# A slot of two heads: attention scores in three passes over halves of the array's rows, queries of both heads in two buffers

## The chip, the cores and the metric

The kernel runs on one core of a Trainium2 chip. The metric is the device time of one execution in microseconds (us), lower is better. All work of the core is done by five engines with queues of their own: TensorE (PE; its weight loads are listed as PEld), VectorE (DVE), ScalarE (ACT), GpSimd (POOL) and SyncE (SP), which here starts most of the DMAs. They wait for each other with semaphores.

## What is computed

One layer of a language-model tower on 8 rows of 512 token numbers. A token's vector comes from a codebook of 2048 rows through a two-layer network (256 to 1024 to 256), so the kernel builds a table of all 2048 rows once. Then for each of the 8 batch rows (cut from the reference; layer norms run over 256 channels, the first 128 are `tok`, the others `pos`):

```python
q, k, v = x_pos @ Wq, x_pos @ Wk, x_tok @ Wv          # 16 heads of 64, 4 heads of keys and values
q = rotate(q, q_phase_angle)                           # a fixed angle for each head
att = q @ k.T / 8 + exp(alibi_log_slopes) * (i - j)    # causal: i >= j
e = exp(att - max(att))
out = (e / (1 + sum(e))) @ v
h = h + out @ Wo
y = layernorm(h)
h = h + gelu((y @ U1) @ V1 + b1) @ U2 @ V2 + b2        # ranks 64, inner width 1024
```

Everything is float32. To keep that precision with the faster `float32r` type, most products split an operand into a high part (rounded to float32r by a copy on ACT) and a low part (the rest, by a subtraction on DVE), called `_hi` and `_lo` here.

## The kernel before

`token_table` builds the table (the first 134 us of the profiled execution). `layer` does the rest: 8 batch rows times 16 heads make 128 head slots, and `SLOTS` adds a few for what lags behind. The order of the work is written out by hand: each engine's program is a loop over slots that calls the same helpers, and lists (`first`, `second`) say which products besides attention fall into which slot: `q` (queries of a pair of heads), `k` (keys for four heads), `x` (turning the positions of the next batch row), and of the batch row before `w` (output product, four tiles of tokens), `y` (turning the normed rows), `u`, `f`, `g`, `d` (the four products of the feed-forward).

A head's scores form a lower triangle of 512 x 512: four tiles of 128 queries against 128, 256, 384 or 512 keys, named by `q` = 0 to 3, in the units `UNITS = ((3,), (2, 0), (1,))`. The steps for a head:

1. `scores` on TensorE, two passes for each tile over all 128 rows. The rows of `q_both` hold the high part of the head's queries in one half and the low part in the other; `k_hi` and `k_lo` hold the keys twice. Units take turns in banks 0 and 1 of PSUM (`RING`, `ring_opened`).
2. `least_of` on DVE (L994) adds mask and position term, writes the result to `probs` and keeps each row's least. `probs` is a ring of three heads.
3. `exps` on ACT (L822), with the sums; `invert` on DVE (L1001); `normalize` on POOL (L783) multiplies all four tiles by the reciprocal.
4. `turn` on TensorE (L1372), ten transposes into banks 2 to 4 (`turn_ps`, one buffer), two slots behind the scores (`LAG`); `move` on ACT (L829) copies them to `turned_sb`.
5. `values` on TensorE (L1388), for two heads at once, in column halves of the array (`tile_position=(0, e * D)`), float32, into bank 5; `o_part` on ACT (L871) and `o_rest` on DVE (L1040) split the result.

Banks 6 (`a_bank`) and 7 (`c_bank`) serve all other products; `before` and `emptied` make each use wait until the one before it has been read. ACT must load another table when it goes from exponentials to gelus and back, which is once a batch row each way. In the text, switching the division of the array means going between products over the whole array, products in column halves and products in row halves. The line numbers in the profile are those of this listing.

## Time and profile before

| | us |
|---|---|
| median of 3 runs | 945.58 |
| lowest, highest | 944.63, 945.79 |
| the profiled execution | 943.51 |
| its span, first to last instruction | 941.7 |
| of it before the first scores | 134 |

The mean granted clock of TensorE was 0.996 of 2.4 GHz. A timeline row gives start, duration, engine, source line, operation and output<-inputs; the shape stands at its end. Recorded durations of TensorE overlap each other, so its pace is read from the distances between starts. A bracket gives the engine's idle time before the row and what ended it.

### The profile page before, as it was taken

How to read it: one execution, taken by the hardware profiler on the slowest of the kernel's cores; microseconds unless marked ns; L12 is line 12 of the kernel's file. 1: busy time of each engine (PE TensorE's matmuls, PEld its weight loads, DVE VectorE, ACT ScalarE, POOL GpSimd, SP SyncE). 2: the span in 40 equal slices, each digit the busy share in tenths (PEclk: the TensorE clock that was granted, in tenths of full speed). 3: DMA queues.
4: the chain of work that ended last, by engine and by line, in shares of the span. 5: the costliest groups of instructions: out<-in, count | busy, mean ns of one | idle time of the engine just before them, and what ended most of it. 6: DMA issues, size and time to landing. Idle time of an engine off the chain costs nothing.

```text
span 941.7 us, 16997 instructions
## 1 busy us (share of the span) xinstructions
PE 872.0 (93%) x5660; PEld 680.4 (72%) x5660; DVE 581.7 (62%) x1779; ACT 728.0 (77%) x1622; POOL 627.7 (67%) x599
## 2 busy tenths in 40 slices
PE   7999978999999998999999999999899999999997
PEld 6888856777866786577766876777667866787585
DVE  5565636776684658475847575756756684658434
ACT  6855348998689869996889688877888689869843
POOL 6000069899686878688767878596868686868630
PEclk9999999999999999999999999999999999999999
DMA  9333360001000200020000100010001000000000
GB/s 262 73 112 112 125 190 1 1 1 56 2 1 1 79 1 2 1 73 7 2 1 24 56 1 1 23 58 1 1 23 57 1 1 1 23 2 1 1 23 23
DMA packets 23605, 33.56 MB, mean 36 GB/s; under 512 B 2608, under 2 KB 20176, under 8 KB 23520
## 3 DMA queue, kind: packets, MB, share of 16 engines
q1 hardware_dynamic: 19760, 19.01, 6.3%
q0 software_dynamic: 3760, 13.48, 5.0%
q8 instruction: 46, 0.75, 0.3%
q14 instruction: 39, 0.32, 0.1%
HBM read 17.80 MB, written 14.68 MB: 34 GB/s over the span
## 4 chain that ended last, share of the span: by engine, by line
PE 49%; ACT 13%; POOL 11%; issue 8%; DVE 6%; DMA 0%; POOLq 0%; DVEq 0%; ACTq 0%
PE ps L1388 12%; PE ps L1192 12%; POOL probs L783 9%; PE ps L1372 8%; PE ps L1360 5%; ACT probs L822 5%; PE ps L1361 4%; ACT turned_sb L829 4%; PE ps L1340 3%; DVE probs L994 2%; POOL token_rows L771 2%; PE ps L1200 1%; ACT k_hi L844 1%; ACT q_both L839 1%; PE ps L1334 1%
## 5 line engine op out<-in xcount | busy, mean ns | idle before, releaser
L783 POOL TENSOR_SCALAR probs<-probs,sums 128x512 f32<-128x512 f32 (+3 forms) x512 | 545.2, 1083 | 155.0 <-DVE sums L1001 154.6
L994 DVE CUSTOM_DVE_ANT_0 probs<-ps,causal,slope 128x512 f32<-128x512 f32 (+3 forms) x512 | 260.0, 547 | 162.0 <-PE ps L1361 161.5
L822 ACT ACTIVATE probs<-probs 128x513 f32<-128x513 f32 (+3 forms) x512 | 283.8, 556 | 34.9 <-DVE probs L994 27.4
L829 ACT ACTIVATE turned_sb<-ps 128x1280 f32<-128x1280 f32 x128 | 157.1, 1228 | 59.3 <-PE ps L1372 59.2
L1360 PE MATMUL ps<-k_hi,q_both 128*128 128x512 f32 (+3 forms) x512 | 181.0, 354 | 19.2 <-DVE probs L994 18.3
L1372 PE MATMUL ps<-ident,probs 128*128 128x128 f32 x1280 | 162.1, 274 | 5.3 <-POOL probs L783 5.3
L1388 PE MATMUL ps<-turned_sb,token_rows 128*64 128x512 f32 (+3 forms) x1024 | 152.0, 438 | 13.5 <-ACT turned_sb L829 13.5
L1361 PE MATMUL ps<-k_lo,q_both 128*128 128x512 f32 (+3 forms) x512 | 152.6, 324 | 0.0
L1372 PEld LDWEIGHTS ps<-ident,probs 128*128 128x128 f32 x1280 | 143.7, 142 | 6.8 <-POOL probs L783 6.5
L1388 PEld LDWEIGHTS ps<-turned_sb,token_rows 128*64 128x64 f32 x1024 | 75.2, 136 | 98.6 <-issue 82.6
L1360 PEld LDWEIGHTS ps<-k_hi,q_both 128*128 128x128 f32 x512 | 96.6, 189 | 61.1 <-DVE probs L994 34.9
L1361 PEld LDWEIGHTS ps<-k_lo,q_both 128*128 128x128 f32 x512 | 97.2, 190 | 4.6
L822 ACT ACTIVATION_READ_ACCUMULATOR probs<-probs 128x1 f32 x512 | 96.0, 188 | 0.0
L1009 DVE TENSOR_TENSOR q_both<-ps,q_both 64x512 fp32r<-64x512 f32 x128 | 88.1, 688 | 9.6 <-ACT q_both L839 6.2
L839 ACT ACTIVATE q_both<-ps 64x512 fp32r<-64x512 f32 x128 | 75.3, 588 | 14.5 <-PE ps L1192 12.8
L261 POOL TENSOR_TENSOR row_guess<-row_var,minus_half 128x4 f32<-128x4 f32 x4 | 4.1, 1026 | 89.8 <-DVE row_var L367 89.8
L1192 PE MATMUL ps<-wo_hi,o_hi 128*128 128x256 f32 x224 | 63.1, 282 | 0.0
L1192 PE MATMUL ps<-wo_lo,o_hi 128*128 128x256 f32 x224 | 62.7, 280 | 0.0
L1192 PE MATMUL ps<-wo_hi,o_lo 128*128 128x256 f32 x224 | 62.7, 280 | 0.0
L1040 DVE TENSOR_TENSOR o_lo<-ps,o_hi 128x512 fp32r<-128x512 f32 x64 | 44.2, 691 | 20.6 <-ACT o_hi L871 19.8
L310 ACT ACTIVATE hid<-ps,b_col 128x512 f32<-128x512 f32 x32 | 22.0, 686 | 28.9 <-PE ps L489 27.5
L415 DVE TENSOR_TENSOR hid_lo<-hid,hid_hi 128x512 fp32r<-128x512 f32 x32 | 22.1, 692 | 34.7 <-ACT hid_hi L315 23.4
(225 smaller groups left out, 1443.9 us busy)
## 6 DMA issues: line engine op xcount, KB each, us to landing
out_dram<-token_rows SPq DMA_DIRECT2D x7, 512.0 KB, 2.9
token_table<-made SPq DMA_DIRECT2D x4, 768.0 KB, 4.0
rows<-in_L_tok_codebook_dram SPq DMA_DIRECT2D x4, 512.0 KB, 9.9
w_f<-in_L_tok_W_dram SPq DMA_DIRECT2D x8, 256.0 KB, 6.1
early_rows<-made SPq DMA_DIRECT2D x4, 512.0 KB, 3.0
early_values<-xn SPq DMA_DIRECT2D x4, 512.0 KB, 3.0
token_table<-xn SPq DMA_DIRECT2D x4, 512.0 KB, 4.8
wo_f<-in_L_attn_Wo_dram POOLq DMA_DIRECT2D x1, 1024.0 KB, 10.3
```

The source lines that it names most:

```text
L783: ins = pool.tensor_scalar(at, at, recip[:, s % P_RING, q:q + 1], None, ALU.mult)
L822: act.activation(at, at, ACT.Exp, bias=least, scale=-1.0, accum_out=sums[:, s % P_RING, q:q + 1]).then_inc(exped, 1)
L829: act.activation(turned_sb[:, s % 2, :], turn_ps, ACT.Copy).then_inc(moved, 1)
L839: act.activation(q_both[at, s % 4, :], a_of("q", n, 0)[at, :], ACT.Copy).then_inc(q_high, 1)
L994: dve.tensor_tensor_reduce(out=probs[:, s % P_RING, start:end], in0=bank(unit % 2)[:, UNIT_AT[q]:UNIT_AT[q] + P * (q + 1)], in1=causal[:, ...
L1009: dve.tensor_tensor(q_both[to, s % 4, :], a_of("q", n, 0)[at, :], q_both[at, s % 4, :].bitcast(F32), ALU.subtract).then_inc(q_low, 1)
L1040: dve.tensor_tensor(o_lo[:, p % O_RING, :], o_bank, o_hi[:, p % O_RING, :].bitcast(F32), ALU.subtract)\
L1192: mm = pe.matmul(dst, w, x, start=n == 0, stop=n == len(parts) - 1)
L1360: pe.matmul(dst, w, k_hi[:, slot, 0:P * (q + 1)], start=True, stop=False)
L1361: mm = pe.matmul(dst, w, k_lo[:, slot, 0:P * (q + 1)], start=False, stop=True)
L1372: mm = pe.transpose(turn_ps[:, K_AT[k] + P * (q - k):K_AT[k] + P * (q - k + 1)], probs[:, s % P_RING, P_AT[q] + P * k:P_AT[q] + P * (k + 1 ...
L1388: mm = pe.matmul(o_bank[rows, P * k:T], v_rows[:, b % 3, k, n // REP * D:(n // REP + 1) * D], turned_sb[:, (s + e) % 2, K_AT[k]:K_AT[k] + ...
```

## The change

A slot now holds a pair of heads (`t`, 64 of them and two behind, indexed j = 0 to 7 within a batch row).

- **Scores.** The two heads of a pair are computed in the two row halves of the array (`tile_position=(e * D, 0)`), 64 rows of contraction each, into bank 0 for one head and bank 1 for the other. Each tile has three passes for each head: high by high, low by high, high by low.
- **Queries.** `q_hi` and `q_lo` hold both heads at once, so a pair has one copy on ACT and one subtraction on DVE over 128 partitions (before: two of each over 64).
- **Banks.** All units write banks 0 and 1, so a unit waits for the minima of the unit before it (both heads). `q`, `x` and some others use bank 6, the rest bank 7; `k` alternates; both halves of `d` use bank 7.
- **Order.** A slot on TensorE is: scores 0, the odd head's turn of two slots ago, `early`, scores 1, the first half of `values`, the even head's turn of the last slot, `middle`, scores 2, the second half of `values`, `late`. `probs` becomes a ring of four heads.
- **Normalizing** is cut up by units, with three reciprocals a pair; the smallest tile goes from POOL to DVE (`normalize_first`). The batch statistics are taken tile by tile after each `w`.
- **Memory.** `xn` and `scratch` now lie in the buffer `ff` of the feed-forward.

The core of the diff:

```diff
-            def scores(s, j):
-                if j == 0:
-                    pe.wait_ge(q_low, s + 1)
-                    pe.wait_ge(k_low, s // REP + 1)
-                ring_opened(("s", s, j))
-                unit = RING_NO["s", s, j]
-                for q in UNITS[j]:
-                    dst = bank(unit % 2)[:, UNIT_AT[q]:UNIT_AT[q] + P * (q + 1)]
-                    w = q_both[:, s % 4, q * P:(q + 1) * P]
-                    slot = s // REP % 2
-                    pe.matmul(dst, w, k_hi[:, slot, 0:P * (q + 1)], start=True, stop=False)
-                    mm = pe.matmul(dst, w, k_lo[:, slot, 0:P * (q + 1)], start=False, stop=True)
+            def scores(t, u):
+
+                if u == 0:
+                    pe.wait_ge(q_low, t + 1)
+                    pe.wait_ge(k_low, t // 2 + 1)
+                    if t >= 1:
+                        pe.wait_ge(biased, 2 * NT * t)
+                    if t >= 1 and burst(t - 1):
+                        pe.wait_ge(ff_made, KF * (t // PAIRS - 1) + 6)
+                else:
+                    pe.wait_ge(biased, 2 * NT * t + UNIT_DONE[u - 1])
+                slot = t // 2 % 2
+                for q in UNITS[u]:
+                    for n, (w, x) in enumerate(((q_hi, k_hi), (q_lo, k_hi), (q_hi, k_lo))):
+                        for e in range(2):
+                            rows = slice(e * D, (e + 1) * D)
+                            mm = pe.matmul(bank(e)[:, UNIT_AT[q]:UNIT_AT[q] + P * (q + 1)], w[rows, t % 2, q * P:(q + 1) * P],
+                                           x[rows, slot, 0:P * (q + 1)], start=n == 0, stop=n == 2, tile_position=(e * D, 0))
                 mm.then_inc(scored, 1)
...
             def turn(s):
                 pe.wait_ge(normed, s + 1)
+                pe.wait_ge(first_normed, s // 2 + 1)
                 if s >= 1:
                     pe.wait_ge(moved, s)
...
+            def minima(t, u):
+
+                dve.wait_ge(scored, len(UNITS) * t + u + 1)
+                for q, e, of in PAIR_ORDER:
+                    if of == u:
+                        s = 2 * t + e
+                        if u == 0 and s >= P_RING:
+                            dve.wait_ge(turned, s - P_RING + 1)
...
+            def after_minima(kind, n, m):
+
+                return kind in "gyd" or kind == "k" and bank_of("k", n, m) is c_bank
...
+            def normalize_first(t):
+
+                dve.wait_ge(recip_done, len(UNITS) * t + 2)
+                for e in range(2):
+                    at = probs[:, (2 * t + e) % P_RING, P_AT[0]:P_AT[0] + P]
+                    ins = dve.tensor_scalar(at, at, recip[:, t % 2, e, SUM_AT[0]:SUM_AT[0] + 1], None, ALU.mult)
+                ins.then_inc(first_normed, 1)
...
+            for t in range(SLOTS):
+                if t < ALL_PAIRS:
+                    exps(t, 0, (0,))
+                if t >= 2:
+                    move(2 * (t - 2) + 1)
+                if t < ALL_PAIRS:
+                    exps(t, 0, (1,))
...
+                for use in early(t):
                     high(*use)
...
+                if t < ALL_PAIRS:
+                    exps(t, 1)
+                for use in middle(t):
+                    high(*use)
+                if t >= 2:
+                    o_part(t - 2)
+                if 1 <= t <= ALL_PAIRS:
+                    move(2 * (t - 1))
+                if t < ALL_PAIRS:
+                    exps(t, 2)
+                for use in late(t):
+                    high(*use)
```

and the new lists of the other products:

```python
def early(t):
    i, j = divmod(t, PAIRS)
    out = []
    if t + 1 < ALL_PAIRS:
        out.append(("q", t + 1, 0))
    if 1 <= i < B and j in (2, 3):
        out.append(("w", i - 1, 2 * (j - 2)))
    return out

def middle(t):
    i, j = divmod(t, PAIRS)
    return [({5: "y", 6: "u", 7: "d"}[j], i - 1, 0)] if 1 <= i < B and j in (5, 6, 7) else []

def late(t):
    i, j = divmod(t, PAIRS)
    out = []
    if t % 2 == 0 and t // 2 + 1 < ALL // REP:
        out.append(("k", t // 2 + 1, 0))
    if i + 1 < B and j == 3:
        out.append(("x", i + 1, 0))
...
        if j in (2, 3):
            out.append(("w", b, 2 * (j - 2) + 1))
        if j == 5:
            out.append(("y", b, 1))
        if j == 6:
...
        if j == 7:
            out.append(("d", b, 1))
    return out
```

TensorE in a plain pair, from the second pass of an even head's first tile, before:

```order
L1361 MATMUL ps<-k_lo,q_both 128x512
L1360 MATMUL ps<-k_hi,q_both 128x384 [waits biased]
L1361 MATMUL ps<-k_lo,q_both 128x384
L1360 MATMUL ps<-k_hi,q_both 128x128
L1361 MATMUL ps<-k_lo,q_both 128x128
L1192 MATMUL ps<-pos_hi,wq_hi 128x512 [waits x_high,k_low]
L1192 MATMUL ps<-pos_hi,wq_lo 128x512
L1192 MATMUL ps<-pos_lo,wq_hi 128x512 [waits x_low]
L1388 MATMUL ps<-turned_sb,token_rows 64x512 [waits moved,o_low]
L1388 MATMUL ps<-turned_sb,token_rows 64x512
L1388 MATMUL ps<-turned_sb,token_rows 64x384 x2
L1388 MATMUL ps<-turned_sb,token_rows 64x256 x2
```

and TensorE's rows after the change, from the first tile of scores 1 of such a pair:

```order
L1366 MATMUL ps<-k_hi,q_hi 128x384 [waits biased]
L1366 MATMUL ps<-k_hi,q_hi 128x384
L1366 MATMUL ps<-k_hi,q_lo 128x384 x2
L1366 MATMUL ps<-k_lo,q_hi 128x384 x2
L1366 MATMUL ps<-k_hi,q_hi 128x128 x2
L1366 MATMUL ps<-k_hi,q_lo 128x128 x2
L1366 MATMUL ps<-k_lo,q_hi 128x128 x2
L1398 MATMUL ps<-turned_sb,token_rows 64x512 [waits moved,o_low]
L1398 MATMUL ps<-turned_sb,token_rows 64x512
L1398 MATMUL ps<-turned_sb,token_rows 64x384 x2
L1379 MATMUL ps<-ident,probs 128x128 [waits moved,first_normed,normed]
L1379 MATMUL ps<-ident,probs 128x128 x9
```

A head's scores were eight passes, six of them in one piece ahead of q and the values; a pair's are now 24 instructions in three pieces, this one of twelve, and the first half of the values follows it at once, in another division of the array.

ACT around the gelus of a batch row, before (the table load and the gelus are L861, the copy of o L871, of the transposes L829):

```order
L822 ACTIVATE probs,sums<-probs 128x129 [waits biased]
L871 ACTIVATE o_hi<-ps 128x512 [waits w_full,valued]
L822 ACTIVATE probs,sums<-probs 128x257 [waits biased]
L861 ACT_TABLE_LOAD [waits ff_used]
L861 ACTIVATE ff<-ps,c_col 128x512 [waits ff_full]
L861 ACTIVATE ff<-ps,c_col 128x512 [waits ff_used,ff_full] x5
L829 ACTIVATE turned_sb<-ps 128x1280 [waits valued,turned]
L861 ACTIVATE ff<-ps,c_col 128x512 [waits ff_used,ff_full] x2
L910 ACT_TABLE_LOAD
```

and after (the copy of u's result is L852, of o L868, of the transposes L829, of k L841, the gelus L858):

```order
L852 ACTIVATE rank_both<-ps 128x512 [waits u_full]
L868 ACTIVATE o_hi<-ps 128x512 [waits w_full,valued]
L829 ACTIVATE turned_sb<-ps 128x1280 [waits valued,turned]
L822 ACTIVATE probs,sums<-probs 128x257 [waits biased] x2
L841 ACTIVATE k_hi<-ps 128x512 [waits scored,k_full]
L858 ACT_TABLE_LOAD [waits ff_used]
L858 ACTIVATE ff<-ps,c_col 128x512 [waits ff_full]
L858 ACTIVATE ff<-ps,c_col 128x512 [waits ff_used,ff_full] x7
```

The copy of the transposes stood between the gelus and stands ahead of them now, with both heads' last exponentials and the copy of k.

## Rows read from the trace of the kernel before

**Rows 1.** The page, busy time, share of the span and instructions.
```profile
PE 872.0 (93%) x5660; PEld 680.4 (72%) x5660; DVE 581.7 (62%) x1779; ACT 728.0 (77%) x1622; POOL 627.7 (67%) x599
```

**Rows 2.** The timeline, one plain pair: start, duration, engine, line, operation, idle before.
```profile
312.33 0.48 PE L1360 MATMUL ps<-k_hi,q_both 128*128 128x512 f32 x1
...
312.65 0.40 PE L1361 MATMUL ps<-k_lo,q_both 128*128 128x512 f32 x1
...
313.19 0.75 DVE L994 CUSTOM_DVE_ANT_0 probs<-ps,causal,slope 128x512 f32<-128x512 f32 x1
...
315.40 0.48 PE L1360 MATMUL ps<-k_hi,q_both 128*128 128x512 f32 x1
...
316.32 0.08 DVE L994 DVE_READ_ACCUMULATOR2_ANT probs<- 128x1 f32 x1
...
316.46 0.44 PE L1360 MATMUL ps<-k_hi,q_both 128*128 128x384 f32 x1 [0.34 <-DVE probs L994]
...
316.95 1.22 ACT L829 ACTIVATE turned_sb<-ps 128x1280 f32<-128x1280 f32 x1
...
318.31 2.38 PE L1388 MATMUL ps<-turned_sb,token_rows 128*64 128x512 f32 x16 [0.32 <-ACT turned_sb L829]
...
321.97 0.48 PE L1360 MATMUL ps<-k_hi,q_both 128*128 128x512 f32 x1
```

**Rows 3.** The timeline of TensorE alone, in the batch row after.
```profile
406.20 0.39 PE L1361 MATMUL ps<-k_lo,q_both 128*128 128x512 f32 x1
406.43 0.34 PE L1360 MATMUL ps<-k_hi,q_both 128*128 128x384 f32 x1
406.61 0.34 PE L1361 MATMUL ps<-k_lo,q_both 128*128 128x384 f32 x1
...
406.84 0.27 PE L1361 MATMUL ps<-k_lo,q_both 128*128 128x128 f32 x1
406.95 0.44 PE L1192 MATMUL ps<-pos_hi,wq_hi 128*128 128x512 f32 x1
...
407.46 0.39 PE L1192 MATMUL ps<-pos_lo,wq_hi 128*128 128x512 f32 x1
407.78 2.38 PE L1388 MATMUL ps<-turned_sb,token_rows 128*64 128x512 f32 x16
410.09 0.39 PE L1360 MATMUL ps<-k_hi,q_both 128*128 128x256 f32 x1
410.31 0.28 PE L1361 MATMUL ps<-k_lo,q_both 128*128 128x256 f32 x1
410.43 1.25 PE L1372 MATMUL ps<-ident,probs 128*128 128x128 f32 x10
411.44 0.48 PE L1360 MATMUL ps<-k_hi,q_both 128*128 128x512 f32 x1
```

**Rows 4.** The page, groups: busy, mean ns of one, then idle time before.
```profile
L783 POOL TENSOR_SCALAR probs<-probs,sums 128x512 f32<-128x512 f32 (+3 forms) x512 | 545.2, 1083 | 155.0 <-DVE sums L1001 154.6
...
L822 ACT ACTIVATE probs<-probs 128x513 f32<-128x513 f32 (+3 forms) x512 | 283.8, 556 | 34.9 <-DVE probs L994 27.4
L829 ACT ACTIVATE turned_sb<-ps 128x1280 f32<-128x1280 f32 x128 | 157.1, 1228 | 59.3 <-PE ps L1372 59.2
...
L1009 DVE TENSOR_TENSOR q_both<-ps,q_both 64x512 fp32r<-64x512 f32 x128 | 88.1, 688 | 9.6 <-ACT q_both L839 6.2
L839 ACT ACTIVATE q_both<-ps 64x512 fp32r<-64x512 f32 x128 | 75.3, 588 | 14.5 <-PE ps L1192 12.8
```

**Rows 5.** The timeline around the feed-forward's gelus, ACT and TensorE.
```profile
382.79 1.28 ACT L861 ACT_TABLE_LOAD   x1
...
384.08 2.42 ACT L861 ACTIVATE ff<-ps,c_col 128x512 f32<-128x512 f32 x4
...
384.92 1.56 PE L1340 MATMUL ps<-ff,u 128*64 128x512 f32 x4 [0.47 <-ACT ff L861]
...
391.78 0.50 PE L1360 MATMUL ps<-k_hi,q_both 128*128 128x512 f32 x1
```

More of the change, by code:

```diff
@@ L648, in layer @@
     spare = g["spare"]
[L649 removed]
+    ff = g["ff"]
     z_hi, z_lo = y_hi[:, 0, :], y_lo[:, 0, :]
@@ new lines, in _ @@
+            for t in range(SLOTS):
+                i, j = divmod(t, PAIRS)
+                if t < ALL_PAIRS:
+                    minima(t, 0)
+                if 1 <= t <= ALL_PAIRS:
+                    invert(t - 1, 2)
+                for use in late(t - 1) if t >= 1 else []:
+                    if after_minima(*use):
+                        low(*use)
+                if 1 <= i < B and j == 4:
+                    norm_front(("y", i - 1))
+                if 1 <= i < B and j == 5:
+                    norm_back(("y", i - 1))
+                for use in early(t):
+                    if use[0] == "w":
+                        low(*use)
+                if t < ALL_PAIRS:
+                    minima(t, 1)
+                    invert(t, 0)
+                for use in early(t):
+                    if use[0] != "w":
+                        low(*use)
+                if t < ALL_PAIRS:
+                    minima(t, 2)
+                    invert(t, 1)
+                    normalize_first(t)
+                for use in middle(t):
+                    low(*use)
+                if t >= 2:
+                    o_rest(t - 2)
+                for use in late(t):
+                    if not after_minima(*use):
+                        low(*use)
+                if 1 <= i < B and j == 4:
+                    norm_root(("y", i - 1))
@@ L1374, in turn, with values @@
                 mm.then_inc(turned, 1)
-            def values(s):
+            def values(s, tiles):
                 b, n = divmod(s, HEADS)
@@ L1383, in values @@
                     pe.wait_ge(o_low, s // 2)
+                if b >= 1 and n == HEADS - 6:
+                    pe.wait_ge(ff_made, KF * b)
                 pe.wait_ge(moved, s + 2)
-                for k in range(NT):
+                for k in tiles:
                     for e in range(2):
@@ L1409, in _ @@
                     filler(bank(1), 4)
-            for s in range(SLOTS):
-                if s < ALL:
-                    scores(s, 0)
-                    scores(s, 1)
-                for use in first(s):
+            for t in range(SLOTS):
+                if t < ALL_PAIRS:
+                    scores(t, 0)
+                if t >= 2:
+                    turn(2 * (t - 2) + 1)
+                for use in early(t):
                     product(*use)
-                if s == ALL:
+                if t < ALL_PAIRS:
+                    scores(t, 1)
+                if t == ALL_PAIRS:
                     last_ahead(0)
-                if 2 + LAG <= s < ALL + 1 + LAG and (s - LAG) % 2 == 0:
-                    values(s - 2 - LAG)
-                if s < ALL:
-                    scores(s, 2)
-                turn_ahead = burst(s) or ("u", s // HEADS - 1, 0) in second(s)
-                if turn_ahead and LAG <= s < ALL + LAG:
-                    turn(s - LAG)
-                for use in second(s):
-                    product(*use)
-                if not turn_ahead and LAG <= s < ALL + LAG:
-                    turn(s - LAG)
-                if s == ALL:
+                if t == ALL_PAIRS + 1:
+                    last_ahead(2, range(PAIRS // 2 - 1))
+                if t >= 2:
+                    values(2 * (t - 2), (0, 1))
+                if 1 <= t <= ALL_PAIRS:
+                    turn(2 * (t - 1))
+                for use in middle(t):
+                    product(*use)
+                if t < ALL_PAIRS:
+                    scores(t, 2)
+                if t >= 2:
+                    values(2 * (t - 2), (2, 3))
+                for use in late(t):
+                    product(*use)
+                if t == ALL_PAIRS:
                     last_ahead(1)
-                if s == ALL + 1:
-                    last_ahead(2, range(PAIRS // 2 - 1))
             last_ahead(2, range(PAIRS // 2 - 1, PAIRS - 2))
```

288 lines of the change are left out of this document (97 added, 191 removed).

## The prediction

> **What bounds the kernel now.** I read the shares first: TensorE is busy for 93% of the span, ACT 77%, DVE 62% [rows 1]. A busy share that high says only that TensorE sets the time on average, so I then read one plain pair of heads in the timeline [rows 2] and the distances between the starts of TensorE's instructions [rows 3].
>
> The distances are what counts, since recorded durations overlap. In [rows 3] a pass of 512 columns takes 0.23 us (406.20 to 406.43), one of 384 takes 0.18 (406.43 to 406.61), one of 256 takes 0.12 (410.31 to 410.43) and one of 128 takes 0.11 (406.84 to 406.95): the small ones go at the pace of their weight load, and I count both at 0.11. The ten transposes take 1.01 (410.43 to 411.44). The 16 products of `values` take 2.31 with the gap behind them (407.78 to 410.09): the two column halves run beside each other. The last q pass before them starts at 407.46 and would be through at 407.69, and the first product starts at 407.78: going into another division of the array costs some 0.1, and the next weight load, which otherwise runs under the pass before, now stands bare (0.05 for 64 columns, 0.11 for 128).
>
> The plain pair of [rows 2] takes 9.64 us (312.33 to 321.97), and its odd head only 3.07 of it. TensorE's own work in such a pair: scores 2 x (0.23 + 0.23 + 2 x 0.18 + 4 x 0.11) = 2.5, transposes 2.2, values 2.3, q 0.7, half of a k 0.35, so 8.1. The other 1.5 us are waits: for the minima of DVE (the 0.34 at 316.46), and for ACT's copy of the transposes (318.31, 0.32 and the drain before it). So TensorE is nearly but not quite the bound; a chain through ACT and DVE runs a bit behind it. POOL's normalizing is next, 8 x 1.083 = 8.7 us a pair [rows 4]. Sixteen heads, one batch row with its output product and feed-forward, take 99.1 us (312.33 in [rows 2] to 411.44 in [rows 3], the same place of two neighbouring rows).
>
> **The scores.** Before: 16 passes a pair over all rows, 2.5 us. After: 24 instructions over 64 rows, which are 12 steps if the two row halves run beside each other: 3 x (0.23 + 0.18 + 0.11 + 0.11) = 1.9 with the same distances. That takes off 0.6 us a pair. No row shows two row halves at once. The nearest are the two column halves of `values`: 16 instructions in 2.3 us (two per step). I take the row halves to run beside each other, loads and passes, and keep the other end (nothing beside anything): 3.8 us, 1.3 more than before.
>
> The Trainium skill, "TensorE: Matmul & The Clock Gate", Part 3 (Packing small matmuls), gives 3.07 times for four row tiles, not 4. By its ratio the steps would take 1.9 / 0.77 = 2.5, an estimate of no gain at all, and the sum would come out some 25 us higher; no row here shows row tiles.
>
> **The switches.** Before, a plain pair changes the division of the array twice, into `values` and out. After, the order of TensorE's rows is scores 0, odd turn, q, scores 1, first half of values, even turn, scores 2, second half of values: seven changes, eight with k. That is five or six more, each 0.1 and a bare load of 0.05 to 0.11, so 0.9 us a pair. The trace shows the price for columns only. Lower end for rows: nothing. With it TensorE's work is 8.1 a pair without k and 8.9 with: no less than before.
>
> The Trainium skill, "TensorEngine Tiling (Array Packing)", Tiling Modes, says "Changing tiling mode (not just tile) drains the TensorE". For columns the trace agrees (the 0.1 above); for rows no run here shows it, and it speaks against this change.
>
> **The new chain.** Scores are now written by turns of both heads into banks 0 and 1, so each unit waits until DVE is through with the last. The second head's minimum in unit 0 also waits until the odd turn has read its place in `probs`, and the odd turn waits for ACT's copy of the even turn, which stands on ACT behind the copy of o, which waits for the second half of values. Round this circle, from the odd turn:
> turn 0.10 + 1.25 recorded [rows 3], and 0.14 until DVE starts (313.05 to 313.19 [rows 2]): 1.49. Minimum of the second head 0.75 and 0.06 until TensorE starts (316.40 to 316.46 [rows 2]): 0.81. Scores 1: 0.11 + 3 x 0.18 + 3 x 0.11 = 0.98. Change and first half of values, 896 of 1280 columns of 2.2 us: 0.10 + 1.55 = 1.65. Change and even turn: 1.21. Change and scores 2: 0.10 + 0.44 = 0.54. Change, second half of values 0.66, drain and signal some 0.25: 1.0. Copy of o 0.59, copy of the turn 1.23 [rows 4], 0.14 until TensorE starts (318.17 to 318.31 [rows 2]): 1.96. Sum 9.64.
> So the plain pair stays at 9.6: what the scores give, bare loads, changes and this circle take back. ACT has 0.6 less (one copy of q for two, L839 in [rows 4]), DVE 0.7 less (L1009), POOL loses its smallest multiply to DVE. None of the three stands alone on the path, so this counts as nothing; if ACT were the bound it would be worth 0.6 a pair.
>
> **The batch row, slot by slot** (j is the slot of two heads, 0 to 7). j = 0, 1: 9.6 each. j = 2 and 3 carry two output products each, 24 passes at 0.11 = 2.7 apiece. They fill the waits, and TensorE's own work counts: 8.9 + 5.4 = 14.3 and 8.1 + 5.4 + 0.5 (x) = 14.0. j = 4: 9.7. j = 5 has the first turn of y inside the circle: 9.6 + 0.5 = 10.1.
> j = 6 is where it loses most. The q product needs bank 6, which the second turn of y has filled. Its copy stands on ACT behind the last exponentials of slot 5, its rest on DVE behind the minima: q starts some 2 us late, and scores 1 at 4.0 instead of 2.3. Then values, turn and u (6 x 0.23): scores 2 at 9.3. From there ACT has the copy of o (ready after 1.5), the turn 1.2, two exponentials 1.1, k 0.6, the table 1.28 and two gelus 1.2 (four took 2.42, [rows 5]), before the first u2 product can start: 9.3 + 7.5 = 16.8. From the first such product to the next scores the trace shows 6.9 (384.92 to 391.78 [rows 5]), with one turn's copy of 1.23 between that is no longer there, so perhaps 6.4; with scores 0, 0.9: 24.1. Before, copies and exponentials stood behind the gelus or ran under values; TensorE now idles some 3 us for them.
> j = 7: both d products use bank 7. The second waits for DVE's addition of the first (0.69), which stands behind the last minima and the new multiply. TensorE waits 1.7 there: 11.6.
> Sum 9.6 + 9.6 + 14.3 + 14.0 + 9.7 + 10.1 + 24.1 + 11.6 = 103.0, 3.9 more than 99.1. Seven rows of the batch have this, 27 us. In the first row, without feed-forward to hide it, DVE sits before slots 3 and 7 waiting for k's copy: 1.5 each, and filling up costs about 1, so 4. The tail has the same products in about the same order; I add 2 for its first waits. In all +33 us. The profiled execution took 943.5 (its span 941.7), the median of the three timed runs is 945.6, 2 above. So 943.5 + 33 + 2 = **979 us**.
>
> **The rivals.**
> (a) A change between whole array and row halves costs nothing and the loads run ahead. Then scores 1 and scores 2 lose their bare loads and one gap, 0.3 a pair in the circle: 64 x 0.3 = 19, so 960. For it: transposes follow passes at once (410.31 is followed by 410.43 [rows 3]). Against: the column change.
> (b) The row halves load or stream one after another. Loads alone: scores 1 gains 3 x (0.22 - 0.18) + 3 x 0.11 = 0.45 and scores 2 0.33, so 0.78 a pair, 50 us: 1029. Passes too: 1.1 a pair, 70 us: 1049. For it: 128-column steps already run at the pace of the load (0.11). Against: `values`.
> (c) Faster. The circle breaks: the copies and hand-overs overlap more than I added up (the drain and signals are 0.7 of it, the entry loads 0.5), and only TensorE's work counts in the six slots without output products. It is then 8.5 instead of 9.6 in the plain ones, and the late y, k and d are partly hidden. The price is -1.1 in some 45 slots, about -50: 930. It decides from the point where circle and late products lose 0.55 us a slot together (33 / 64 and more). For it: ACT and DVE have less work, and it takes small errors only. Against: each link is a row.
> That the change doesn't do what it says (row halves side by side) is the upper end of (b).
>
> **How the numbers follow.** My sum has 45%, and covers 965 to 1000. (a) 14%, 950 to 965. (c) 25%, 905 to 943. (b) 16%, 1015 to 1055. The range that leaves out no more than 2 in 10 cuts (c) in its middle and the upper half of (b): 925 to 1035. A measurement of this kernel can tell about 0.2% from no change. Faster 25%, the same 3%, slower 72%.
>
> **What would show it.** In the profile after: pairs of score products a few ns apart at steps of 0.23, 0.18 and 0.11 (else (b)); a gap of 0.1 with a bare load at each change (else (a)); plain slots at 9.6 with TensorE waiting before the odd turn for ACT's copy, and before scores 1 for DVE; some 3 us of waiting for gelus in slot 6, and 1.7 for bank 7 in slot 7; sixteen heads in 103 us. It is wrong if plain slots come below 9.0 (then (c)), or if the time is right and slots 5 to 7 do not lose.

## The result and the profile after

| | before | after |
|---|---|---|
| median, us | 945.68 (944.63 to 945.97, 4 runs) | 977.03 (976.79 to 977.35, 4 runs) |
| the profiled execution, its span | 943.51, 941.7 | 977.22, 975.4 |
| mean granted clock | 0.996 | 0.989 |

The ratio is 1.0337 [1.0324, 1.035]: 31 us slower, 33.7 in the spans. Where they lie, from the starts of `scores` 0 of the first slots of each batch row: the scores begin at 132.94 (before 133.96), -1.0 (each part as after minus before). The first row takes 76.9 (before 73.7), +3.2. The six rows behind it take 106.07, 103.77 and four times 102.27 against 99.1 before, +24.1. The last row up to its last slot takes 91.4 (before 86.3), +5.2, and what remains takes 55.25 (before 52.96), +2.3.

So each middle row loses 3.2 us, and two of them lose 5.3 more between them. The page of after, answering to [rows 1] (busy time, share, instructions):

```profile
PE 888.8 (91%) x6172; PEld 634.4 (65%) x6172; DVE 572.7 (59%) x1907; ACT 669.4 (69%) x1558; POOL 558.6 (57%) x471
```

Every engine but TensorE has less to do than before (ACT 59 us less, POOL 69 less, DVE 9 less), and the kernel is slower all the same.

A plain slot, TensorE's timeline (columns as in [rows 2]), answering to [rows 2, 3]. It is slot j = 1, from its `scores` 0 to the first turn of the slot behind it; x2 are the two row halves:

```profile
531.15 0.50 PE L1366 MATMUL ps<-k_hi,q_hi 64*128 64x512 f32 x2
531.48 0.40 PE L1366 MATMUL ps<-k_hi,q_lo 64*128 64x512 f32 x2
531.72 0.40 PE L1366 MATMUL ps<-k_lo,q_hi 64*128 64x512 f32 x2
532.24 1.28 PE L1379 MATMUL ps<-ident,probs 128*128 128x128 f32 x10
...
534.37 0.44 PE L1366 MATMUL ps<-k_hi,q_hi 64*128 64x384 f32 x2 [0.16 <-DVE probs L989]
...
535.17 0.27 PE L1366 MATMUL ps<-k_lo,q_hi 64*128 64x128 f32 x2
535.52 1.72 PE L1398 MATMUL ps<-turned_sb,token_rows 128*64 128x512 f32 x8
537.18 1.31 PE L1379 MATMUL ps<-ident,probs 128*128 128x128 f32 x10
538.42 0.39 PE L1366 MATMUL ps<-k_hi,q_hi 64*128 64x256 f32 x2
538.65 0.28 PE L1366 MATMUL ps<-k_hi,q_lo 64*128 64x256 f32 x2
538.76 0.28 PE L1366 MATMUL ps<-k_lo,q_hi 64*128 64x256 f32 x2
538.97 0.87 PE L1398 MATMUL ps<-turned_sb,token_rows 128*64 128x256 f32 x8
540.13 0.50 PE L1366 MATMUL ps<-k_hi,q_hi 64*128 64x512 f32 x2 [0.28 <-DVE probs L989]
...
541.76 0.30 PE L1379 MATMUL ps<-ident,probs 128*128 128x128 f32 x1 [0.67 <-ACT turned_sb L829]
```

The row halves do run side by side: in the single records the two of a pair start 3 ns apart, and the pairs follow each other by 0.24 (531.48 to 531.72) and 0.11 (538.65 to 538.76), as single passes did before [rows 3]. The idle time before `scores` 1 (0.16, for DVE's minimum) and before the odd turn (0.67, for ACT's copy) stands where the prediction put it. The wait of `scores` 0 behind the second half of values, for the minima of `scores` 2, is not a link of the circle that it added up.

The chain of work that ended last, over the same stretch (start, us, what); "issue" is time in which the engine waited for nothing that the profile shows:

```profile
532.24 1.30 PE ps L1379 x10
...
533.56 0.77 DVE probs L989 x2
...
534.37 1.07 PE ps L1366 x12
...
535.52 1.72 PE ps L1398 x8
537.25 1.25 PE ps L1379 x10
538.50 0.55 PE ps L1366 x6
539.04 0.82 PE ps L1398 x8
...
539.91 0.47 issue
540.39 1.24 ACT turned_sb L829
...
541.76 1.28 PE ps L1379 x10
```

This is the circle of the prediction, link by link: odd turn, minimum, scores 1, first half of values, even turn, scores 2, second half, copy of o (0.47 of "issue" in this view; ACT's timeline has the copy start at 539.89), copy of the turn, odd turn. It takes 541.76 - 532.24 = 9.52 us, where I had added up 9.64.

The groups of after (busy, mean ns of one, idle before), answering to [rows 4]. POOL now has three multiplies a head, the smallest tile is DVE's, and the copy of o is the place where ACT waits:

```profile
L780 POOL TENSOR_SCALAR probs<-probs,sums 128x512 f32<-128x512 f32 (+2 forms) x384 | 476.5, 1257 | 264.4 <-DVE sums L999 263.8
...
L868 ACT ACTIVATE o_hi<-ps 128x512 fp32r<-128x512 f32 x64 | 38.3, 598 | 90.6 <-PE ps L1398 90.6
...
L1010 DVE TENSOR_SCALAR probs<-probs,sums 128x128 f32<-128x128 f32 x128 | 42.5, 441 | 2.3
```

Slot 6 of the same row, TensorE and then ACT, answering to [rows 5]:

```profile
590.30 1.28 PE L1379 MATMUL ps<-ident,probs 128*128 128x128 f32 x10 [0.44 <-ACT turned_sb L829]
593.09 0.50 PE L1192 MATMUL ps<-pos_hi,wq_hi 128*128 128x512 f32 x1 [1.52 <-DVE y_lo L1033]
...
602.67 0.47 PE L1334 MATMUL ps<-rank_both,v_hi 128*128 128x512 f32 x1 [1.05 <-DVE rank_both L1036]
...
604.74 0.50 PE L1334 MATMUL ps<-rank_both,v_hi 128*128 128x512 f32 x1 [0.90 <-DVE k_lo L1020]
...
606.10 1.56 PE L1340 MATMUL ps<-ff,u 128*64 128x512 f32 x4 [0.17 <-ACT ff L858]
...
612.81 0.50 PE L1366 MATMUL ps<-k_hi,q_hi 64*128 64x512 f32 x2
```
```profile
600.77 0.60 ACT L868 ACTIVATE o_hi<-ps 128x512 fp32r<-128x512 f32 x1 [0.77 <-PE ps L1398]
...
603.37 0.59 ACT L841 ACTIVATE k_hi<-ps 128x512 fp32r<-128x512 f32 x1
603.98 1.28 ACT L858 ACT_TABLE_LOAD   x1
```

TensorE stands still for 1.52, 1.05 and 0.90 us here. The view of waits sums these over all seven feed-forwards (total, times, longest); its second row is `d` in slot 7:

```profile
PE ps L1192 <- DVE y_lo L1033: 10.6, 7, 1.5
PE ps L1192 <- DVE token_rows L1045: 9.8, 7, 1.4
...
PE ps L1334 <- DVE rank_both L1036: 8.2, 7, 1.9
PE ps L1334 <- DVE k_lo L1020: 5.4, 6, 0.9
```

The two rows that took 106.07 and 103.77 differ from the others mainly in slot 6: 26.98 and 25.41 us instead of 23.92, 4.6 of the 5.3. (The other 0.7 is the first slot of the longer one, 9.92 instead of 9.20, at full clock.) Stretches of after (length, then busy time of PE, PEld, DVE, ACT, POOL, the granted clock, DMA share, GB/s): slot 6 of two rows, and two pieces of the first of them:

```profile
277.50:304.50 27.00, 22.92 (x105) 12.22 (x104) 9.80 (x30) 19.01 (x39) 10.67 (x9) 0.87 0.00 1
588.90:612.80 23.90, 19.82 (x105) 10.81 (x104) 9.76 (x30) 18.93 (x39) 10.64 (x9) 1.00 0.00 1
```
```profile
277.50:282.00 4.50, 2.54 (x18) 1.83 (x18) 3.55 (x10) 4.50 (x11) 3.99 (x4) 0.96 0.02 4
282.00:285.00 3.00, 3.00 (x15) 2.23 (x15) 0.00 (x0) 1.37 (x4) 1.01 (x2) 0.50 0.00 0
285.00:288.00 3.00, 3.00 (x10) 0.77 (x8) 2.37 (x10) 2.08 (x8) 0.91 (x1) 0.50 0.00 0
```

The same 105 matmuls take 3.1 us longer: after TensorE has idled 1.5 us for `y_lo` (its first q product starts at 281.73 there), its clock is granted at 0.50, 1.2 GHz, for more than six us. The same happens in slot 6 of the last row (24.89 us at a mean of 0.93).

### The profile page after: what moved, and what is told of

Same layout as the page of the kernel before. It is cut to its first block, busy times and chain, and to the rows that moved or that the text cites. A ratio compares the mean times of both kernels' runs of the same rounds, so it can differ in the third digit from the quotient of the medians.

```text
span 975.4 us, 17527 instructions
## 1 busy us (share of the span) xinstructions
PE 888.8 (91%) x6172; PEld 634.4 (65%) x6172; DVE 572.7 (59%) x1907; ACT 669.4 (69%) x1558; POOL 558.6 (57%) x471
## 4 chain that ended last, share of the span: by engine, by line
PE 66%; ACT 9%; DVE 7%; issue 5%; DMA 0%; POOL 0%; POOLq 0%; ACTq 0%; DVEq 0%
PE ps L1398 16%; PE ps L1379 15%; PE ps L1192 14%; PE ps L1366 13%; ACT turned_sb L829 5%; DVE probs L989 4%; PE ps L1340 3%; ACT probs L822 2%; PE ps L1334 1%; ACT L858 1%; PE ps L1335 1%; PE ps L1200 1%; ACT k_hi L841 1%; ACT ff L858 0%; PE ps L1271 0%
## 5 line engine op out<-in xcount | busy, mean ns | idle before, releaser
L780 POOL TENSOR_SCALAR probs<-probs,sums 128x512 f32<-128x512 f32 (+2 forms) x384 | 476.5, 1257 | 264.4 <-DVE sums L999 263.8
L1398 PE MATMUL ps<-turned_sb,token_rows 128*64 128x512 f32 (+3 forms) x1024 | 167.8, 448 | 3.5 <-ACT turned_sb L829 2.6
L829 ACT ACTIVATE turned_sb<-ps 128x1280 f32<-128x1280 f32 x128 | 157.4, 1229 | 2.4 <-PE ps L1379 2.4
L1366 PE MATMUL ps<-k_hi,q_hi 64*128 64x512 f32 (+3 forms) x512 | 101.0, 390 | 14.7 <-DVE probs L989 12.1
L868 ACT ACTIVATE o_hi<-ps 128x512 fp32r<-128x512 f32 x64 | 38.3, 598 | 90.6 <-PE ps L1398 90.6
L1366 PEld LDWEIGHTS ps<-k_hi,q_hi 64*128 64x128 f32 x512 | 49.2, 188 | 69.7 <-issue 33.6
L1366 PE MATMUL ps<-k_hi,q_lo 64*128 64x512 f32 (+3 forms) x512 | 84.4, 325 | 0.0
L1366 PE MATMUL ps<-k_lo,q_hi 64*128 64x512 f32 (+3 forms) x512 | 84.2, 323 | 0.0
L1366 PEld LDWEIGHTS ps<-k_lo,q_hi 64*128 64x128 f32 x512 | 50.0, 191 | 2.6
L1366 PEld LDWEIGHTS ps<-k_hi,q_lo 64*128 64x128 f32 x512 | 50.1, 191 | 0.0
L1010 DVE TENSOR_SCALAR probs<-probs,sums 128x128 f32<-128x128 f32 x128 | 42.5, 441 | 2.3
## 6 DMA issues: line engine op xcount, KB each, us to landing
rows<-in_L_tok_codebook_dram SPq DMA_DIRECT2D x4, 512.0 KB, 10.1
```

The lines of the kernel that those rows point to most:

```text
L780: ins = pool.tensor_scalar(at, at, recip[:, t % 2, e, SUM_AT[q]:SUM_AT[q] + 1], None, ALU.mult)
L829: act.activation(turned_sb[:, s % 2, :], turn_ps, ACT.Copy).then_inc(moved, 1)
L868: act.activation(o_hi[:, p % O_RING, :], o_bank, ACT.Copy).then_inc(o_high, 1)
L1010: ins = dve.tensor_scalar(at, at, recip[:, t % 2, e, SUM_AT[0]:SUM_AT[0] + 1], None, ALU.mult)
L1366: mm = pe.matmul(bank(e)[:, UNIT_AT[q]:UNIT_AT[q] + P * (q + 1)], w[rows, t % 2, q * P:(q + 1) * P], x[rows, slot, 0:P * (q + 1)], start=n ...
L1398: mm = pe.matmul(o_bank[rows, P * k:T], v_rows[:, b % 3, k, n // REP * D:(n // REP + 1) * D], turned_sb[:, (s + e) % 2, K_AT[k]:K_AT[k] + ...
```

## The experiments

Three questions: are row halves what was counted (e1, e2, e12), is the circle the bound (e3, e8, e9), and do the late products and DVE's order cost what was counted (e4 to e7, e10, e11)? Each ratio is to the kernel before on the same chip, whose medians were 944.3 to 946.2. "A row" is a batch row in the middle, at full clock.

**e1: the same order, whole array.** The twelve steps of a pair stay, but each is one pass over all 128 rows.

```diff
-                        for e in range(2):
-                            rows = slice(e * D, (e + 1) * D)
-                            mm = pe.matmul(bank(e)[:, UNIT_AT[q]:UNIT_AT[q] + P * (q + 1)], w[rows, t % 2, q * P:(q + 1) * P],
-                                           x[rows, slot, 0:P * (q + 1)], start=n == 0, stop=n == 2, tile_position=(e * D, 0))
+                        mm = pe.matmul(bank(n % 2)[:, UNIT_AT[q]:UNIT_AT[q] + P * (q + 1)], w[:, t % 2, q * P:(q + 1) * P],
+                                       x[:, slot, 0:P * (q + 1)], start=n < 2, stop=n > 0)
```

> Each step of the scores is one pass over all 128 rows instead of two passes over 64 rows: 12 instructions a pair, same order, same waits. The scores are then sums over both heads, so the output is not the reference's; what it leaves out is only the division by rows. If the division costs what I put down (a gap of 0.10 to 0.15 and a bare weight load of 0.11 at each change, three pieces a slot), about 0.37 us a slot goes from the circle and some 0.2 more in the slots that TensorE fills: 25 us less, 952. If a change to row halves is free or hidden: 975 or more.

Measured 957.32, ratio 1.0127 [1.0106, 1.0149]: 20 us below after. A row takes 99.35 (after 102.27), so 0.36 a slot in the mean of the eight (0.1 to 0.75 in the single ones). TensorE's timeline around `scores` 2 shows where:

```profile
519.91 0.36 PE L1364 MATMUL ps<-k_hi,q_hi 128*128 128x256 f32 x1
520.11 0.28 PE L1364 MATMUL ps<-k_hi,q_lo 128*128 128x256 f32 x1
520.23 0.28 PE L1364 MATMUL ps<-k_lo,q_hi 128*128 128x256 f32 x1
520.44 0.87 PE L1396 MATMUL ps<-turned_sb,token_rows 128*64 128x256 f32 x8
```

The last transpose before them starts at 519.88, 0.03 ahead. In after it starts at 538.22 and `scores` 2 at 538.42, 0.20 behind it, with 0.23 to the second pass instead of 0.20. Out to the column halves it is 0.21 in both (538.76 to 538.97, 520.23 to 520.44). So here going into the row halves costs 0.20 where it costs 0.03 between whole-array products, and going on to the column halves costs nothing more. In five of the six middle rows of e1 slot 6 takes 24.6 to 25.2 us instead of 23.7, the clock again, which is part of why it came out 5 us over my 952. Rival (a), that this change of division is free, is refuted, and the step of the prediction that charged it is shown. How much of the 0.20 is a drain of the array and how much a bare weight load, no run here divides.

**e2: row halves, one after another.** Both heads use the first 64 rows, so nothing can run side by side.

```diff
-                            rows = slice(e * D, (e + 1) * D)
+                            rows = slice(0, D)
...
-                                           x[rows, slot, 0:P * (q + 1)], start=n == 0, stop=n == 2, tile_position=(e * D, 0))
+                                           x[rows, slot, 0:P * (q + 1)], start=n == 0, stop=n == 2, tile_position=(0, 0))
```

> Both heads' passes use the same row half, so the two passes of a step cannot run beside each other; the output is not the reference's (the second head's scores are the first's). If TensorE's links are on the circle: scores 1 gains 0.87 and scores 2 0.33 in every slot, scores 0 0.7 in the slots that TensorE fills: 85 to 90 us more, 1065. If ACT or POOL were the bound and TensorE only near it: under 30 more, below 1007.

Measured 1108.49, ratio 1.1745 [1.1706, 1.1785]; TensorE's timeline:

```profile
606.29 0.70 PE L1366 MATMUL ps<-k_hi,q_hi 64*128 64x512 f32 x2 [0.28 <-DVE probs L989]
606.83 0.62 PE L1366 MATMUL ps<-k_hi,q_lo 64*128 64x512 f32 x2
607.28 0.61 PE L1366 MATMUL ps<-k_lo,q_hi 64*128 64x512 f32 x2
```

A pair now takes 0.45 (606.83 to 607.28) where side by side it took 0.24. The total is 131 us above after, where I expected 88. The slots' lengths divide it. Where each is at full clock, the eight slots of a middle row take 11.12, 10.57, 16.56, 16.23, 11.10, 11.24, 25.32 and 13.61, together 115.75 us, 13.5 more than in after; for eight rows that is some 108, an estimate. The other 23 or so are the clock: its mean is 0.962, slot 6 takes up to 28.6 us and slot 0 up to 14.0. That the halves run side by side in after is settled: rival (b), and with it "the change doesn't do what it says", is refuted. Its price of 70 us would have been too low.

**e12: the same order, whole array, as many passes as before.** Each head has two passes, 16 a pair.

```diff
-                    for n, (w, x) in enumerate(((q_hi, k_hi), (q_lo, k_hi), (q_hi, k_lo))):
-                        for e in range(2):
...
+                    for e, w in enumerate((q_hi, q_lo)):
+                        for n, x in enumerate((k_hi, k_lo)):
+                            mm = pe.matmul(bank(e)[:, UNIT_AT[q]:UNIT_AT[q] + P * (q + 1)], w[:, t % 2, q * P:(q + 1) * P],
+                                           x[:, slot, 0:P * (q + 1)], start=n == 0, stop=n == 1)
```

> The new order with passes as they were before: for each head and tile two passes over all 128 rows, 16 a pair, no division by rows. The operands are not those of the kernel before (the passes take q_hi or q_lo of both heads), so the output is not the reference's; count, widths and banks of the passes are the old ones. Against the 12 whole passes of the first experiment (957.3) a pair has 0.63 us more of passes. If these are on the path as its 0.37 was: 957 + 30 = 987, so that dividing by rows does pay, by 10. If the changes of division eat the whole gain of the third pass: 977, the time of the changed kernel. If less than half is on the path: under 970.

Measured 978.85, ratio 1.0355 [1.0323, 1.0386], a row 102.67. Together with e1 it divides the change into its parts, for a row of sixteen heads:

| | a row | step |
|---|---|---|
| before | 99.11 | |
| the new order, 16 passes, whole array (e12) | 102.67 | +3.6 |
| 12 passes, whole array (e1) | 99.35 | -3.3 |
| 12 steps in row halves (after) | 102.27 | +2.9 |

The scores in row halves are worth -0.4 us a row, nothing: four passes fewer give 0.41 a slot, and the division takes back 0.36. What makes the kernel slower is what came with them: the order, with the banks, the merged queries and the divided normalizing, which e12 keeps and does not tell apart.

**e3: the circle cut.** The transposes get three places instead of two, so that the copy of the turn needn't wait for the second half of values, and it goes ahead of the copy of o.

```diff
-                if s >= 2:
-                    act.wait_ge(valued, s - 1)
-                act.activation(turned_sb[:, s % 2, :], turn_ps, ACT.Copy).then_inc(moved, 1)
+                if s >= 3:
+                    act.wait_ge(valued, s - 2)
+                act.activation(turned_sb[:, s % 3, :], turn_ps, ACT.Copy).then_inc(moved, 1)
...
-                if t >= 2:
-                    o_part(t - 2)
                 if 1 <= t <= ALL_PAIRS:
                     move(2 * (t - 1))
+                if t >= 2:
+                    o_part(t - 2)
```

> turned_sb has three places instead of two, and ACT copies the even head's transposes before o. This opens the circle odd turn, minimum, scores 1, values, even turn, scores 2, values, copy of o, copy of the turn. If the circle is the bound of the plain slots: they go from 9.0-9.2 to about 8.5, the gelu slot loses another 1.2, together 30 us less, 947. If something else bounds them (DVE's minima, POOL), within 5 of 977.

Measured 953.14, ratio 1.011 [1.0079, 1.0141], 24 us below after (the profiled execution is its fastest, 949.9). The circle cost that much. Slots of a row, `scores` 0 to `scores` 0:

| j | 0 | 1 | 2 | 3 | 4 | 5 | 6 | 7 | row |
|---|---|---|---|---|---|---|---|---|---|
| after | 9.20 | 8.98 | 15.34 | 14.33 | 9.34 | 9.75 | 23.92 | 11.40 | 102.27 |
| e3 | 9.20 | 8.67 | 14.62 | 14.35 | 9.22 | 9.85 | 22.56 | 11.40 | 99.87 |

Cut like this, the plain slots seem to give only 0 to 0.3 and slot 2 0.7; but the 0.67 of waiting before the odd turn, which ends the circle of slot 1, falls behind `scores` 0 of slot 2. From odd turn to odd turn slots 0, 1 and 4 give 0.2, 0.85 and 0.3 (9.40, 9.52, 9.53 to 9.23, 8.67, 9.20), slot 2 nothing and slot 6 0.85. The first row gives 5.5 (71.4, at a mean clock of 1.00 where after has 0.96), and no slot 6 falls to the lower clock, which is worth 5 more.

**e8: `probs` a ring of six heads** (`P_RING = 6`; before the change three, after it four), which takes away the minimum's wait for the odd turn. **e9: e3 and e8 together.**

> The changed kernel with six places in probs instead of four, so that the second head's minimum no longer waits for the odd turn. The earlier runs showed two circles of nearly one length in the plain slots (9.2 and 9.0 us): one through ACT's copies, one through DVE (scores 0, odd turn, second head's minimum, scores 1, last minima, scores 0). Both hold the link cut here. If so, some 0.3 a slot goes until ACT's copy holds alone: 965 to 970. If the second circle isn't one: within 2 of 977.

> Both circles cut: three places in turned_sb with the copy moved up, six in probs. With turned_sb alone the plain slots stayed at 9.2 and 8.7 (953 in all). If the circle through DVE was what took over, they fall by some 0.5 more, in about 40 slots: 930. If DVE's or POOL's own load is what is left: 950 or more.

e8: 975.11, ratio 1.0324 [1.0305, 1.0342]; 2 us instead of 7 to 12, and slot 1 stays at 8.99. With every slot at full clock its row would be 101.6, 0.7 below after, but at the end of every second row the clock falls (415 to 419, 620 to 624, 825 to 828): slot 7 and the slot 0 behind it take 0.4 to 0.5 and 0.9 to 1.1 longer. e9: 949.23, ratio 1.0055 [1.0034, 1.0076]; a row 99.1, plain slots 9.03 and 8.50. That is not the 930 of the second circle, and near the 950 that I had put down to DVE's or POOL's own load, but not for that reason. With both links cut, two slots of e9 read like this (columns as in the stretches above), and then the `scores` 0 that ends the second of them:

```profile
504.60:522.10 17.50, 17.25 (x130) 11.49 (x129) 12.12 (x45) 14.93 (x37) 12.63 (x11) 1.00 0.09 31
```
```profile
522.13 0.50 PE L1366 MATMUL ps<-k_hi,q_hi 64*128 64x512 f32 x2 [0.28 <-DVE probs L989]
```

TensorE is busy for 17.25 of 17.50 us. DVE (12.1) and POOL (12.6) are not the bound. In the slot with k TensorE has no idle time: 9.03 us are its own work. The slot without k ends with the wait of 0.28 us for the minima of `scores` 2, since the next `scores` 0 writes the same banks. It is the link that none of the experiments cuts: after has it in the same place (0.28 at 540.13), and e7, e10 and e11 too. Without it that slot would be some 8.2 us, an estimate.

**e4: the two turns of y change banks**, so that `q` in slot 6 doesn't wait for y's rest.

```diff
-    y_bank = (c_bank, a_bank)
+    y_bank = (a_bank, c_bank)
...
-        if kind in "qx" or (kind, m) in (("y", 1), ("f", 2), ("f", 6)) or kind == "k" and n % 2 == 0:
+        if kind in "qx" or (kind, m) in (("y", 0), ("f", 2), ("f", 6)) or kind == "k" and n % 2 == 0:
```

> The first turn of y goes to bank 6 and the second to bank 7, so that the q product of slot 6 no longer waits for the second's rest. If that wait (1.5 us a batch row, seven of them) is on the path: 10.5 less, and up to 4 more where the granted clock fell in that slot: 963 to 967. If slot 6 is bound by ACT before the gelus anyway: within 2 of 977.

Measured 972.75, ratio 1.0306 [1.0277, 1.0336], 4 us instead of 10 to 14. Slot 6 does fall by 1.4, to 22.5, in two middle rows; in the four behind them the clock takes 0.9 of it back (stretches of slot 6 in the second row, in a later one, and a piece of the later):

```profile
281.60:304.10 22.50, 19.70 (x105) 10.87 (x104) 9.84 (x30) 18.77 (x39) 10.03 (x9) 1.00 0.00 1
586.90:610.30 23.40, 20.77 (x107) 11.11 (x106) 9.82 (x30) 18.79 (x39) 10.01 (x9) 0.93 0.00 1
```
```profile
602.00:605.00 3.00, 3.00 (x7) 0.75 (x6) 0.00 (x0) 2.31 (x4) 0.00 (x0) 0.51 0.00 0
```

The clock falls there right behind the waits of 1.05 and 0.90 us for the rests of u and k. Slot 5 gives back another 0.6 (9.75 to 10.34), where the first turn of y now waits for the rest of q. And the first row takes 80.4 us (after 76.9), with two slots at a mean clock of 0.84, which hides another 3.5.

**e5: DVE takes the rest of y, u and d before the last minima.**

```diff
+                for use in middle(t):
+                    low(*use)
                 if t < ALL_PAIRS:
                     minima(t, 2)
...
-                for use in middle(t):
-                    low(*use)
```

> On DVE the rest of the middle product (y, u, d) stands before the last minima of the slot instead of behind them and the multiply. If slot 7's second d product waits for it (1.4 us) and slot 6's first v1 product too (1.05, of which the minima keep half): 13 less, 964. If something else is late there: within 2 of 977.

Measured 973.35, ratio 1.0305 [1.0278, 1.0332], 4 us instead of 13. Slot 7 gives its 1.47 (11.40 to 9.93): the wait for bank 7 is shown. Slot 5 loses 0.55, since the rest of y moved ahead of minima that are due, and slot 6 takes 24.8 to 25.0 in all six middle rows, each at a mean clock of 0.93. In that slot the wait for u's rest (`rank_both`) is gone, and this is what stands there:

```profile
601.31 0.50 PE L1334 MATMUL ps<-rank_both,v_hi 128*128 128x512 f32 x1 [1.83 <-DVE k_lo L1020]
```

Most of the idle time (1.05 and 0.90 in after) only moved on, to the rest of k, which stands behind ACT's copy of k. So DVE's order explained the place of the first wait, not the time at which the feed-forward can go on.

**e6: the smallest tile back on POOL**, the other way round.

> Undoes one part: the smallest tile is multiplied on POOL again, not on DVE. I counted it as nothing. It takes 0.9 us a pair from DVE and gives POOL 1.2; neither is on the circle: within 2 of 977. If DVE's queue sets the plain slots: 5 to 30 less. If POOL does: more.

Measured 977.02, ratio 1.0345 [1.0318, 1.0371]: no difference from after in the total, as expected. The slots say more. Slot 7 takes 10.85 instead of 11.40, since the multiply no longer stands on DVE ahead of the rest of d that frees bank 7 (the view of waits, against 9.8, 7, 1.4 in after):

```profile
PE ps L1196 <- DVE token_rows L1050: 6.0, 7, 0.9
```

Four of the six middle rows pay this back in slot 6, 24.7 to 24.8 us at a mean clock of 0.93 where after has 23.92. A row at full clock takes 101.7, 0.5 less than in after. So the multiply is off the path in the plain slots (9.20, 8.99 and 9.33, as in after), and on it in slot 7.

**e7: e3, e4 and e5 together. e10: and six heads in `probs`. e11: as e10, but the rest of y stays behind the last minima.**

> turned_sb with three places and the copy moved up, y's banks swapped, and DVE's middle rests before the last minima. If the three losses are separate links, they add up: 30 + 12 + 13, so 922, which would be below the kernel before (945.7). If they hide each other: 935 to 950.

> The kernel with three edits (936.7) and six places in probs. Separate links: 20 less, 916. If the links hide each other: 930 or more.

> As the one before, but the rest of y's first turn stays behind the last minima on DVE; only u's and d's stand before them. With three edits slot 5 had grown from 9.75 to 10.75 us, since y's rest holds up the minima. If that is why: 0.5 a batch row less, 3.5 below the run before it. If slot 5 grew by the wait for bank 6 alone: no difference.

| | median | ratio | a row |
|---|---|---|---|
| e7 | 936.66 | 0.9913 [0.9895, 0.993] | 97.85 |
| e10 | 931.58 | 0.9858 [0.9839, 0.9878] | 97.0 |
| e11 | 930.05 | 0.9839 [0.9815, 0.9863] | 96.63 |

The three edits of e7 gave 24, 4 and 4 alone and give 40 together: with all of them no slot 6 of a middle row is at the lower clock. At full clock the parts do add up in slots 6 and 7: slot 6 takes 21.1, which is 23.92 less the 1.36 of e3 and the 1.4 of e4, and slot 7 the 9.93 of e5. e7 and e10 came out 15 us above the values for links that add up (922 and 916) and within what I had put down for links that hide each other. In e11 slot 5 returned 0.45 us a row (10.70 to 10.25) as expected; the medians of e10 and e11 are 1.5 apart, where I expected 3.5, and their intervals overlap. e11 is the fastest kernel here, 1.6% below the kernel before: the new division into slots is worth something once most of its waits are gone.

## Why the prediction came out right

**The sum.** Predicted 979 us and 103.0 a row; measured 977.0, and 102.27 at full clock. Measured from odd turn to odd turn, as the prediction did (the row that starts at 521.94):

| j | 0 | 1 | 2 | 3 | 4 | 5 | 6 | 7 | row |
|---|---|---|---|---|---|---|---|---|---|
| predicted | 9.6 | 9.6 | 14.3 | 14.0 | 9.7 | 10.1 | 24.1 | 11.6 | 103.0 |
| measured | 9.40 | 9.52 | 14.62 | 14.33 | 9.53 | 10.05 | 23.41 | 11.40 | 102.27 |

Seven rows were charged 3.9 each; the plain excess is 3.2, so some 5 us too much. What I left out, the clock, put back 4.6 in two middle rows and some in the last, so a part of the closeness is luck: two errors that cancel. The first row was to lose 4 and lost 3.2, the tail 2 and lost 2.3.

**The scores.** Side by side, loads too, at the old distances: right (e2 shows the other case). The 0.6 us taken off was too large by a third: four whole passes less gave 0.41 a slot (e12 against e1).

**The changes of division.** I charged 0.1 and a bare load each, 0.9 us a pair for all. Into the row halves it is 0.20 at `scores` 2. With e9, where less waits, `scores` 0 and 1 start 0.32 behind the 512-column pass before them (513.31 to 513.63, 516.14 to 516.46) where whole passes follow each other after 0.23. The first step of `scores` 0 takes 0.34 to the next and the turn follows its last step after 0.33; e1 has 0.24 for both. The first step of `scores` 1 takes 0.28 in e1 and in e9, so that one is not the row halves'. Together that is some 0.6 of TensorE's time a slot for the row halves alone, an estimate, of which 0.36 shows in the slot (e1). The charge was right in kind and size. By the rule that I quoted from the Trainium skill, "TensorEngine Tiling (Array Packing)", Tiling Modes, a change of mode drains the array; the 0.20 against 0.03 of after and e1 agrees with it for rows, where before I had columns only. The other rule, the 3.07 from "TensorE: Matmul & The Clock Gate", Part 3, is for four row tiles and does not carry over to two halves: passes of 512 columns in pairs go at 0.24 against 0.23 for one before.

**The circle.** Right in its links and in its sum, 9.52 against 9.64, with two terms off by 0.17 that cancel: from the odd turn to DVE's start it took 1.32 (predicted 1.49), `scores` 1 took 1.15 (0.98); the others are within 0.1. Counted from `scores` 0, slot 1 takes 8.98, under the 9.0 that the prediction named as a sign against it; but the wait that closes the circle falls into slot 2 that way, and from odd turn to odd turn no plain slot is below 9.40. TensorE's own work was nearly right too: 9.03 measured in e9 with k (predicted 8.9), and some 8.2 without (8.1). The small rest lies in first passes: 0.28 to 0.34 to the next where I counted 0.18 to 0.23, though [rows 2] has it (312.33 to 312.65 is 0.32). What I did not add up is what comes next once the circle is cut: the wait of `scores` 0 for the last minima, 0.28 in the plain slot without k. And two of the three plain slots of a row carry k, so they had little to give. From odd turn to odd turn e9 takes 0.4, 1.0 and 0.5 off slots 0, 1 and 4, where (c) had 1.1 for each.

**Slots 5 to 7.** Right in place, partly wrong in reason. Slot 7 waited 1.4 us for bank 7 (predicted 1.7; e5 removes it). In slot 6 `q` idled 1.5 for y's rest. The three us of idle time ahead of the gelus were 1.05 + 0.90 + 0.17 = 2.1. I had put them down to ACT's list from the copy of o to the gelus. The row of the wait for the gelu shows 0.17 alone; the others are for DVE's rests of u and k, which I had not named. But the rest of k hangs on ACT's copy of k, which stands in that list (603.37 above), and with u's wait gone the idle time was nearly the same (1.83 in e5). So the list did set it, and the trace names what stopped TensorE on the way. From `scores` 2 to the first product of the gelus it is 6.8 us (599.30 to 606.10; predicted 7.5), from there to the next scores 6.7 (predicted 6.4). Against before, in pairs from `scores` to `scores`, slots 0 to 4 took 57.2 (before 56.7) and slots 5 to 7 45.1 (before 42.4): as expected, the row's loss is where the late products are.

**The rivals.** (a) and (b) are refuted by e1 and e2. (c), that the circle breaks and 930 results, is not what this kernel does. Its price of 50 us was for the circle and the late products together, and together they do give it: the circle alone 24 (e3), with the second link 28 (e9), with the late products 47 (e11, 930).

**Nothing for ACT, DVE and POOL** held for the total: they lost 59, 9 and 69 us of work and the kernel is slower. In the plain slots e6 bears it out. In slot 7 the new multiply on DVE costs 0.55 us a row (e6); the prediction had it in the wait there.

**Left out: the clock.** The mean of 0.996 gave no sign of it before. After, it is some 5 us in three slots 6. In e4, e5, e6 and e8 it took back a part of the gain, and its absence is most of the 8 us by which e7 beats the sum of its parts. That last step is read from the slots' lengths and clocks, not from a run of its own. Why the clock fell in slot 6 of three rows of after and not in the four between, which have the same waits, stays open.

## What to carry to other kernels

Before packing an array's rows, count how often the order enters the packed form: here the three entries a slot cost 0.36 us net, nearly the 0.41 that the saved passes gave, because the scores had been cut into three pieces. Add up the circle of waits, but ask also which wait is left once it is cut, here one of 0.28 us, and how little room TensorE's own work leaves. Cut a slot at the link that closes the circle, or its gain shows up in the neighbour. A gain of one us where TensorE idles may be taken back by its clock, so compare slots at the same granted clock and try such edits together before judging them alone.

## What was unexpected in the hardware

- The granted clock fell from 2.4 to 1.2 GHz for three to over six us behind idle pieces of 1.5 us (after, 282 to 288), or of 1.05 and 0.90 us (e4, 602 to 605), with TensorE 91% busy over the span; rows with the same instructions and waits kept 2.4 GHz.
- Two row halves, float32r, 64 rows each: starts 3 ns apart, 0.24 us for a pair of 512-column passes; on the same half they take 0.45. Into row halves from transposes 0.20 us instead of 0.03, out to column halves 0.21 as from the whole array.
- A multiply of a 128x128 tile by a column is recorded with 441 ns on DVE (after) and 611 on POOL (e6); back on POOL it gave 0.55 us a row in slot 7, where DVE was late, and nothing in the plain slots.
